# Small transposes of an attention kernel lose their PSUM bank and take turns in the rotation of the maxima's banks

## The reference

```python
# attention a: 16 heads of 16, causal, the weights times a decay of the lag after the softmax
att = softmax(where(causal, q @ k.T / 4, -inf))
att = att * decay_weight_matrix(T)        # 1 for lags under 15, falls to 0 at lag 511
y = (att @ v) @ W_proj
# feed forward: weights as signs times their row's mean magnitude, GELU between
# attention b: the same softmax without decay, biases, and a layernorm of its own result
# the same feed forward again
```

## Time and profile before

| what | us |
|---|---|
| median of 3 runs | 2897.58 |
| lowest, highest | 2890.86, 2901.36 |
| the profiled execution | 2902.22 |
| its span | 2900.5 |
| PE busy | 2509.8 (87%) |
| DVE busy | 1989.0 (69%) |
| ACT busy | 1550.1 (53%) |
| POOL busy | 924.4 (32%) |
| att_a's first maximum to its last product matmul | 173.4 to 1193.9 |
| att_b's first maximum to its last product matmul | 1637.8 to 2589.0 |

### The profile page before, as it was taken

How to read it: one execution, slowest core, us unless ns; L and a number is a source line. 1 busy time by engine, 2 the same in 40 slices (tenths; PEclk the granted TensorE clock), 3 DMA queues, 4 the chain that set the end, 5 groups by cost and what they waited for, 6 DMA issues and landing times. The chain is left out here.

```text
span 2900.5 us, 45085 instructions
## 1 busy us (share of the span) xinstructions
PE 2509.8 (87%) x14016; PEld 1451.1 (50%) x14016; DVE 1989.0 (69%) x4919; ACT 1550.1 (53%) x3394; POOL 924.4 (32%) x1108
## 2 busy tenths in 40 slices
PE   4859999999999999566978699999999999965498
PEld 3534545445454554255755355555555555524377
DVE  5567777777777777044656587878778778706665
ACT  1217667685776767212432056666666666651244
POOL 0037778777777787500000200010010100112100
PEclk8969999999999999887989699999999999987799
DMA  4994235052332500495329951350431522019622
GB/s 146 277 148 63 42 53 69 21 85 37 54 57 37 85 9 9 60 181 142 102 68 277 176 81 34 60 82 20 77 53 37 85 43 50 12 25 156 172 90 73
DMA packets 195001, 242.97 MB, mean 84 GB/s; under 512 B 25297, under 2 KB 119378, under 8 KB 194002
## 3 DMA queue, kind: packets, MB, share of 16 engines
q1 hardware_dynamic: 177874, 223.36, 39.6%
q10 hardware_dynamic: 16896, 16.78, 1.9%
HBM read 143.99 MB, written 95.03 MB: 82 GB/s over the span
## 5 line engine op out<-in xcount | busy, mean ns | idle before, releaser
L706 POOL TENSOR_TENSOR att_a_wd<-att_a_wt,decay 128x256 f32<-128x256 f32 (+3 forms) x896 | 755.3, 873 | 255.9 <-PE att_a_po L898 142.6
L745 ACT ACTIVATE att_b_wt<-att_b_ps 128x512 f32<-128x512 f32 (+3 forms) x1280 | 595.1, 538 | 342.4 <-PE att_b_ps L873 338.4
L782 DVE TENSOR_REDUCE att_a_mpart<-att_a_pm 128x1 f32<-128x512 f32 x768 | 509.7, 687 | 145.8 <-PE att_a_pm L847 143.7
L782 DVE TENSOR_REDUCE att_b_mpart<-att_b_pm 128x1 f32<-128x512 f32 x768 | 503.1, 686 | 136.5 <-PE att_b_pm L847 135.0
L745 ACT ACTIVATE att_a_wt<-att_a_ps 128x512 f32<-128x512 f32 (+3 forms) x896 | 437.4, 507 | 216.6 <-PE att_a_ps L876 139.3
L847 PE MATMUL att_a_pm<-att_a_kop,att_a_qop 128*128 128x512 f32 (+3 forms) x1280 | 510.9, 421 | 40.0 <-DMA att_a_qop<-att_a_qop 29.3
L847 PE MATMUL att_b_pm<-att_b_kop,att_b_qop 128*128 128x512 f32 (+3 forms) x1280 | 496.0, 407 | 28.8 <-DMA att_b_qop<-att_b_qop 28.3
L873 PE MATMUL att_b_ps<-att_b_qop,att_b_kop 128*128 128x512 f32 (+3 forms) x1280 | 450.8, 382 | 5.1 <-ACT att_b_wt L745 3.4
L847 PEld LDWEIGHTS att_a_pm<-att_a_kop,att_a_qop 128*128 128x128 f32 x1280 | 239.1, 194 | 291.0 <-DVE att_a_mpart L782 118.5
L847 PEld LDWEIGHTS att_b_pm<-att_b_kop,att_b_qop 128*128 128x128 f32 x1280 | 245.3, 194 | 262.1 <-DVE att_b_mpart L782 109.0
L724 POOL TENSOR_SCALAR_AFFINE_SELECT att_b_wt<-att_b_wt 128x512 f32<-128x512 f32 x128 | 81.5, 637 | 860.1 <-ACT att_b_wt L745 860.1
(11 more groups left out here) (189 smaller groups left out, 2626.8 us busy)
## 6 DMA issues: line engine op xcount, KB each, us to landing
att_a_kop<-qk SPq DMA_DIRECT2D x128, 128.0 KB
att_a_qop<-qk SPq DMA_DIRECT2D x128, 128.0 KB
att_b_kop<-qk SPq DMA_DIRECT2D x128, 128.0 KB
att_b_qop<-qk SPq DMA_DIRECT2D x128, 128.0 KB
qk<-qkv_a_qk_hi SPq DMA_DIRECT2D x32, 256.0 KB, 4.8
qk<-qkv_a_qk_lo SPq DMA_DIRECT2D x32, 256.0 KB, 4.3
v<-qkv_a_vt SPq DMA_DIRECT2D x32, 256.0 KB, 3.9
att_a_va<-v SPq DMA_DIRECT2D x8, 1024.0 KB, 12.3
```

What stands on the lines that cost most here:

```text
L706: pool.tensor_tensor(wd[:, kq % 2, j, a:z], wt[:, kq % buffers, j, a:z], keep["decay"][:, u:u + z - a], ALU.mult).then_inc(w_decayed, 1)
L745: act.activation(wt[:, kq % buffers, j, a:CH], pe_[:, seen % EBANKS, 0:CH - a], ACT.Exp)\
L782: dve.tensor_reduce(mpart[:, c, piece, u:u + 1], pm[:, n % MBANKS, 0:w], AX.X, ALU.max, negate=True).then_inc(m_reduced, 1)
```

## The change

The bank `px` is given up. `MBANKS, EBANKS` are 4 and 3 in both attentions: att_a gets a third bank for scores, att_b a fourth for maxima. A list `TURNS` holds, in the plan's order, every user of the `pm` banks (M, MT, FT), and turn k uses bank k % 4. So a small transpose takes one bank of the rotation from its matmul until VectorE has copied it, and each user waits for that one turn that had its bank before, four turns back: a maximum's reduction, a far piece's exponential, or a transpose's copy. The constants that filled the semaphores for the first round go away. `m_costs` and `m_order` hold what stood in `attention_plan`; costs, order and spacing stay as they were.

```diff
@@ -450,6 +450,24 @@
     return range(max(0, c - 1) if decayed else 0)
+def m_costs(decayed):
+
+    m, n = [], 0
+    for c in range(NC):
+        units = []
+        for qb in range(TB):
+            for j in range(GH):
+                for piece in range(c + 1):
+                    units.append((60.0 + (CH if piece < c else P * (qb + 1)), ("M", n, c, qb, j, piece)))
+                    n += 1
+        m += units + [(0.0, ("MF", c))]
+    return spaced(m, decayed)
+
+
+def m_order(decayed):
+    return [item for _, item in m_costs(decayed)]
+
+
 def attention_plan(weights, rest, ahead, decayed):
...
@@ -548,7 +557,7 @@
         qop = sb("qop", [P, 2, GH, T], F32R)
         va = sb("va", [P, 2, BLOCKS, GH, STRIP], F32)
         buffers = 4
-        MBANKS, EBANKS = (4, 2) if decayed else (3, 3)
+        MBANKS, EBANKS = 4, 3
         wt = sb("wt", [P, buffers, GH, CH], F32)
         wd = sb("wd", [P, 2, GH, CH], F32) if decayed else None
         mpart = sb("mpart", [P, NC, NC, UNITS], F32)
...
@@ -560,7 +569,7 @@
             fsum, ffactor = (sb(n, [P, NC, NC - 2, UNITS], F32) for n in ("fsum", "ffactor"))
             ftotal, frow = sb("ftotal", [P, NC, UNITS], F32), sb("frow", [UNITS, NC - 2, P], F32)
         y = sb("y", [P, 2, CH], F32)
-        pm, pe_, po, px = ps("pm", [P, MBANKS, CH]), ps("ps", [P, EBANKS, CH]), ps("po", [P, CH]), ps("px", [P, CH])
+        pm, pe_, po = ps("pm", [P, MBANKS, CH]), ps("ps", [P, EBANKS, CH]), ps("po", [P, CH])
         qk_in = [[sm(f"qk_in{i}{c}") for c in range(NC)] for i in range(2)]
         m_in = [sm(f"m_in{c}") for c in range(NC)]
...
@@ -602,19 +611,25 @@
             return X_USES * g + c + sum(f < c for f in FARS) + of_sums
-        def far_left(n):
-
-
-            def is_far(k):
-                per = [UNITS * (c + 1) for c in range(NC)]
-                k %= M_UNITS
-                for c in range(NC):
-                    if k < per[c]:
-                        return k % (c + 1) in far(c, decayed)
-                    k -= per[c]
-
-            k = n - MBANKS
-            return sum(is_far(i) for i in range(k + 1)) if k >= 0 else -sum(is_far(i) for i in range(k + 1, 0))
+        TURNS = []
+        fars = 0
+        for item in m_order(decayed):
+            if item[0] == "M":
+                is_far = item[5] in far(item[2], decayed)
+                TURNS.append(("M", item[1], fars if is_far else None))
+                fars += is_far
+            if item[0] in ("MT", "FT"):
+                TURNS.append((item[0], item[1], None))
+        TURN = {turn[:2]: k for k, turn in enumerate(TURNS)}
+
+        def bank_of(g, what, index):
+
+            return (len(TURNS) * g + TURN[what, index]) % MBANKS
+
+        def last_in_bank(g, what, index):
+
+            before = len(TURNS) * g + TURN[what, index] - MBANKS
+            return (-1, (None, None, None)) if before < 0 else (before // len(TURNS), TURNS[before % len(TURNS)])
         def pad(eng, t, par, padded):
...
@@ -747,9 +761,10 @@
                         seen += 1
                     if item[0] == "FX":
                         _, d, n, c, qb, j, piece = item
-                        act.wait_ge(m_reduced, M_UNITS * (g + d) + n + 1 + MBANKS)
+                        bank = bank_of(g + d, "M", n)
+                        act.wait_ge(m_reduced, M_UNITS * (g + d) + n + 1)
                         u = TB * j + qb
-                        act.activation(pm[:, n % MBANKS, :], pm[:, n % MBANKS, :], ACT.Exp,
+                        act.activation(pm[:, bank, :], pm[:, bank, :], ACT.Exp,
                                        bias=mpart[:, c, piece, u:u + 1],
                                        accum_out=fsum[:, c, piece, u:u + 1]).then_inc(f_done, 1)
                     if item[0] == "FE":
...
@@ -776,20 +790,21 @@
                     if item[0] == "M":
                         _, d, n, c, qb, j, piece = item
                         w = CH if piece < c else P * (qb + 1)
+                        bank = bank_of(g + d, "M", n)
                         dve.wait_ge(m_scores, M_UNITS * (g + d) + n + 1)
                         u = TB * j + qb
                         if piece < c:
-                            dve.tensor_reduce(mpart[:, c, piece, u:u + 1], pm[:, n % MBANKS, 0:w],
+                            dve.tensor_reduce(mpart[:, c, piece, u:u + 1], pm[:, bank, 0:w],
                                               AX.X, ALU.max, negate=True).then_inc(m_reduced, 1)
                         else:
-                            dve.tensor_tensor_reduce(out=pm[:, n % MBANKS, 0:w], in0=pm[:, n % MBANKS, 0:w],
+                            dve.tensor_tensor_reduce(out=pm[:, bank, 0:w], in0=pm[:, bank, 0:w],
                                                      in1=keep["late"][:, CH - w:CH], scale=-1.0, scalar=-2 * MASK,
                                                      op0=ALU.add, op1=ALU.min,
                                                      accum_out=mpart[:, c, piece, u:u + 1]).then_inc(m_reduced, 1)
...
@@ -811,18 +826,28 @@
                         _, d, c = item
                         dve.wait_ge(x_written, x_use(g + d, c, 1) + 1)
                         dve.wait_ge(f_out[c], 16 * (g + d + 1))
-                        dve.tensor_copy(frow[:, FARS.index(c), :], px[0:UNITS, 0:P]).then_inc(x_read, 1)
+                        dve.tensor_copy(frow[:, FARS.index(c), :], pm[0:UNITS, bank_of(g + d, "FT", c), 0:P]).then_inc(x_read, 1)
                     if item[0] == "MC":
                         _, d, c = item
                         dve.wait_ge(x_written, x_use(g + d, c, 0) + 1)
                         dve.wait_ge(m_in[c], M_DMAS * (g + d + 1))
-                        dve.tensor_copy(mrow[:, c, :], px[0:GH * TB, 0:P]).then_inc(x_read, 1)
+                        dve.tensor_copy(mrow[:, c, :], pm[0:GH * TB, bank_of(g + d, "MT", c), 0:P]).then_inc(x_read, 1)
             steps(dve, step)
         @block.tensor
         def _(pe):
             pe.sem_inc(pv_done, buffers)
+
+            def wait_bank_free(g, what, index):
+                g, (what, index, far_index) = last_in_bank(g, what, index)
+                if what == "M" and far_index is not None:
+                    pe.wait_ge(f_done, FAR_UNITS * g + far_index + 1)
+                elif what == "M":
+                    pe.wait_ge(m_reduced, M_UNITS * g + index + 1)
+                elif what is not None:
+                    pe.wait_ge(x_read, x_use(g, index, what == "FT") + 2)
+
             def step(g, i, par, plan):
                 e = kq = ones = masked = 0
                 for item in plan:
...
@@ -838,11 +863,8 @@
                                 pe.wait_ge(q_padded[1], c + 1)
                             pe.wait_ge(qk_in[mpar][c], QK_LOADS * (before + 1))
                         w = CH if piece < c else P * (qb + 1)
-                        bank = n % MBANKS
-
-                        pe.wait_ge(m_reduced, M_UNITS * (g + d) + max(n + 1, MBANKS))
-                        if FARS:
-                            pe.wait_ge(f_done, FAR_UNITS * (g + d) + far_left(n) + MBANKS)
+                        bank = bank_of(g + d, "M", n)
+                        wait_bank_free(g + d, "M", n)
                         q0 = c * CH + qb * P
                         mm = pe.matmul(pm[:, bank, 0:w], qop[:, mpar, j, q0:q0 + P],
                                        kop[:, mpar, j, piece * CH:piece * CH + w], start=True, stop=True)
...
@@ -850,14 +872,14 @@
                     if item[0] == "MT":
                         _, d, c = item
                         pe.wait_ge(m_final, NC * (g + d) + c + 1)
-                        pe.wait_ge(x_read, x_use(g + d, c, 0) + 1)
-                        pe.matmul(px[0:GH * TB, 0:P], mneg[:, c, :], keep["ident"][:, :], start=True, stop=True)\
+                        wait_bank_free(g + d, "MT", c)
+                        pe.matmul(pm[0:GH * TB, bank_of(g + d, "MT", c), 0:P], mneg[:, c, :], keep["ident"][:, :], start=True, stop=True)\
                           .then_inc(x_written, 1)
                     if item[0] == "FT":
                         _, d, c = item
                         pe.wait_ge(f_total, len(FARS) * (g + d) + FARS.index(c) + 1)
-                        pe.wait_ge(x_read, x_use(g + d, c, 1) + 1)
-                        pe.matmul(px[0:UNITS, 0:P], ftotal[:, c, :], keep["ident"][:, :], start=True, stop=True)\
+                        wait_bank_free(g + d, "FT", c)
+                        pe.matmul(pm[0:UNITS, bank_of(g + d, "FT", c), 0:P], ftotal[:, c, :], keep["ident"][:, :], start=True, stop=True)\
                           .then_inc(x_written, 1)
                     if item[0] == "S":
                         _, c, kb, j = item
```

More of the change, by code:

```diff
@@ L450, in far @@
     return range(max(0, c - 1) if decayed else 0)
+def m_costs(decayed):
[11 more added lines that the diff above has]
+    return [item for _, item in m_costs(decayed)]
 def attention_plan(weights, rest, ahead, decayed):
-    e, m = [], []
+    e = []
```

(17 more changed lines are left out.)

## The result

| | before | after |
|---|---|---|
| median, us | 2899.47 (6 runs) | 2917.39 (6 runs) |
| lowest to highest | 2890.81 to 2904.12 | 2910.83 to 2920.69 |
| profiled execution, us | 2902.22 | 2910.83 |
| its span, us | 2900.5 | 2908.8 |
| first to last maximum matmul, att_a | 975.2 | 993.8 |

What follows compares the result with a forecast made beforehand. TensorE's in-order queue was taken to set the pace of both attentions. Added waits of 24.4 + 6.3 + 2.6 = 33.3 us, less gains of 9.0 + 4.5, gave +19.8 us: 2917 us, range 2894 to 2934.

Steps and rivals of the forecast that it cites:

- Late copies in att_a, +24.4, and its fill, +1.3: att_a: maxima wait for transposes' copies, 0.55, 0.72, 1.33 and 0.61 us in a group; in the fill VectorE waits.
- steps 3 and 4: att_a, far sums and chunk 2: far exponentials delay maxima ahead of the copy; fourth maximum 1.33 and 0.61 us late.
- Score bank, -9.0: att_a: a third score bank removes each group's score wait, 5.8 us, and smaller weight-load waits; -9.0 us.
- Late copy in att_b, +6.3, and its fill, +1.3: att_b: chunk 2's copy makes a maximum 0.79 us late in 8 groups; in the fill VectorE waits.
- Fourth bank in att_b, -4.5: att_b: a fourth maxima bank removes some four short waits per group, 0.55 us together; -4.5 us.
- The rival of the longer lead: att_a scores, att_b maxima: late weight loads gain 47 us, change -14 us, 2884; chance 0.14.
- Second wait of each maximum, 0: att_a: dropping each maximum matmul's second wait, 65 us at most in TensorE's sequencer, was costed at nothing.
- The clock: Rival, att_a: the new 1.33 us wait lowers TensorE's clock in each group; +33 us, 2931; chance 0.13.
- the absorbed one: Rival: TensorE's other waits, as at the far sums' transpose, take up 60% of 33 us; no change, 2897; chance 0.18.
- The rule of the Trainium skill: PSUM banks: rotate independent matmuls through all eight; a bank serving only small transposes is better given to the rotations.

Runs made afterwards that it cites:

- a_share42: Against the kernel before: att_a's transposes share the maxima's four banks, without the third score bank (4+2), att_b keeps own 3+3; 2928.52 us, ratio 1.0103.
- b_only: Against the kernel before: the change in att_b alone (shared 4+3), att_a keeps own 4+2; 2901.82 us, ratio 1.0001.
- b_copy4: Against the kernel before: att_b shared 4+3, att_a own 4+2, copies at 4 and 15 in place of 6 and 17; 2885.76 us, ratio 0.996.
- own_copy4: Against the kernel before: transposes keep their own bank in both attentions, copies at 4 and 15 in place of 6 and 17; 2901.84 us, ratio 1.002.
- b33_copy4: Against the kernel before: att_b shared 3+3 (7 banks), att_a own 4+2, copies at 4 and 15 in place of 6 and 17; 2894.45 us (1 run).
- a_only: Against the kernel before: the change in att_a alone (shared 4+3), att_b keeps own 3+3; 2918.94 us, ratio 1.0077.

## Why the prediction was right

The time was forecast at 2917, +19.8 us, and came at 2917.39, +17.9. That the two times agree within half a microsecond is luck: three more runs moved before's median from 2897.58 to 2899.47. Term by term:

- *Late copies in att_a, +24.4, and its fill, +1.3*: a_share42 gives 25.5 to 27.3. The single places, each from its transpose to the fourth maximum, came at 0.55 (0.55 forecast) for chunk 0, 0.72 (0.72) for chunk 1, 1.31 (1.33) for the far sums and 0.59 (0.61) for chunk 2: 3.2 us together, against the 3.1 by which a group grew. The ordering read from the trace was right: VectorE's in-order queue drains TensorE's lead. The heading "late copies" covers too much: 1.3 of the 3.1 us stay with early copies. They are the waits for far exponentials that steps 3 and 4 reckoned with.
- *Score bank, -9.0*: 8.6. Of the 9.0 only 5.8 were read from a row; the rest was a choice between two bounds, and came out well. The wait at 586 is gone in each group. The row of weight loads fell from 51.3 to 27.9 us:

```profile
L895 PEld LDWEIGHTS att_a_ps<-att_a_qop,att_a_kop 128*128 128x128 f32 x896 | 169.3, 189 | 66.9 <-issue 29.3 <-ACT att_a_wt L759 27.9
```

- *Late copy in att_b, +6.3, and its fill, +1.3*: b_only against b_copy4 gives 902.8 - 894.7 = 8.1. Chunk 2's came at 0.80 (0.79). The fill has no run of its own; the one place read there kept VectorE idle for 0.89 us, against 0.65 in the forecast.
- *Fourth bank in att_b, -4.5*: **mis-sized**. It brings 11.9 to 13.4 us. The step that failed was "near nothing, since the rest lies under other matmuls": I counted only maxima that stood visibly late. The waits of the weight loads fell by 23.7 us as 11.9 us were won. For att_b this makes 8.1 - 11.9 = -3.8 in place of the +3.1 of my sum. Early copies cost some 1.4 us by themselves with own banks (906.6 against 905.0 to 905.3), which the 8.1 leaves out: -2.4, and the stretch shows -1.7 to -2.5. So the forecast had the wrong sign for att_b, by some 5 us, and att_a came 0.2 to 2 us over its +16.7. The total is right because att_a decides it and because the error in att_b was within the range. The rival of the longer lead was right in kind here and reached half of its size: 8.6 and 11.9 to 13.4 us, where it needed 42.
- *Second wait of each maximum, 0*: right within 0.1 us in a group. The att_a of b_only, own_copy4, b_copy4 and b33_copy4 keeps its own bank and has the single wait; its groups without a clock fall take 123.1 or 123.5 to 123.6 us, against 123.1 to 123.2 or 123.7 before (by the two lengths of the wait at the far sums' transpose).
- *The clock*: the new 1.46 us between two maxima did not make it fall. The clock is 1.00 behind the one shown above (first row). It fell at a group's end only, in two of seven groups after as in two before (second row, after):

```profile
620.00:625.00 5.00, 4.11 (x28) 1.93 (x26) 3.41 (x8) 4.42 (x11) 4.27 (x5) 1.00 1.10 123
...
663.00:668.00 5.00, 4.01 (x19) 2.02 (x19) 2.21 (x13) 1.10 (x3) 0.98 (x2) 0.68 0.01 3
```

  So that rival fell, and so did the absorbed one: the wait at the far sums' transpose kept its two lengths, 1.05 and 1.5 us, with the new waits and without them.
- *The rule of the Trainium skill* ("Perfetto Trace Analysis", "Matmul Optimizations", all eight banks): the kernel uses eight banks both before and after, so the rule didn't decide here; how long a transpose holds a bank did. Where a run leaves a bank unused, the traces agree with the rule: the eighth bank brings 8.6 us in att_a (a_share42 to a_only) and 13.4 in att_b (b33_copy4 to b_copy4).

## What to carry to other kernels

When two kinds of work rotate through the same banks, look at what stands in the reader's in-order queue between a bank's write and the release: if the next user of the bank comes right behind that release, the writer's lead is gone. Place the release early, or leave one more turn between, before the bank is counted as a gain. Then count the turns once more for the slowest reader, here the far exponentials: the small user takes a turn from it wherever its copy stands. And price a further buffer not by the long waits alone: where the weight loads of in-order matmuls wait often, a part of those waits may be time, and TensorE's idle time doesn't show it. Only the length of a group does.

## What the runs showed of the hardware

From the end of a VectorE copy to the start of the matmul that waits for it: 0.06 us (576.42 to 576.48); from that matmul's start to the reduction that waits for it: 0.54 us (576.48 to 577.02). Such a round trip is paid at each handover once the lead is zero. In the fill, at the lower clock, the second step took 0.83 us (1661.73 to 1662.56).

TensorE stops twice at the end of each group of att_a, for about 1.18 us and then for 1.05, for about 1.27 (the two kernels with five banks), or for 1.5. In the thirteen traces the second stop was 1.5 us long 33 times, and the clock went to its lower level behind 11 of these, for 3.4 us each; behind the 58 shorter ones it never did. A longer stop costs a group 0.4 to 0.5 us and a fall some 1.5 to 1.6 more (125.7 to 127.3 us in the changed kernel). The same att_a had seven long stops and two falls in the changed kernel's trace, one and none in a_only's, so the program doesn't fix it; what does was not tried. That makes a single profiled execution uncertain by some 2 us for each.
